# ScalarE's quad copies write four runs of one pixel each instead of two runs of pixel pairs

## The chip, the cores and the metric

The kernel runs on one core of one Trainium2 chip. The metric is device time in microseconds (us), the median of several runs. A profile of one more execution gives the rows that are read here. In it PE is TensorE (PEld its weight loads), DVE is VectorE, ACT is ScalarE, POOL is GpSimd and SP is SyncE, whose queue issues most transfers.

## The reference, cut to what matters

128 images of 3 x 224 x 224 are cut into 8 x 8 patches of 28 x 28 pixels. Every patch is projected to 128 features, gets a position factor, then a windowed attention and a mixture of 16 experts. The change lies in the first step:

```
patches = X.reshape(B, C, 8, 28, 8, 28)
patches = patches.transpose(0, 2, 4, 1, 3, 5).reshape(B, 64, 3 * 28 * 28)
tokens = jnp.einsum('bpi,hi->bph', patches, W) + b          # W: 128 x 2352
...
h = h + attention(layernorm(h)); h = h + moe_and_ffn(layernorm(h))
```

All of it is float32.

## The kernel before, in words

There are three stages. Stage 1 (to about 450 us of the trace) makes tokens, attention and routing for 16 groups of 512 tokens (8 images each); stage 2 runs the experts, stage 3 the last feed-forward layer. The change touches stage 1 alone.

In stage 1 SP loads a group's pixels into `region`, with 84 partitions for the 28 rows of 3 channels and the patch's 28 pixel columns along the free dimension. VectorE moves blocks of the last 7 columns onto unused partitions (`move_block`, L947), so that 21 columns are left to multiply (`MAIN`). For TensorE the 21 columns must be apart, one operand of 256 tokens for each column. ScalarE does that, for each half of a group (256 tokens): `copy_units` writes five quads of four neighbouring columns into `xf` (L632, 128 x 1024 elements each) and the last column into `xlast` (L635, 128 x 256). So a group takes 10 quad copies and 2 copies of a last column. Each such unit raises `xact_ready`.

TensorE's `patch` (L1435) waits for a unit and multiplies each of its columns with that column's weights `wp[:, s]`, adding up over 21 columns in PSUM. The trace has two records of 128x256 for each float32 product, so a quad is 8 records and a last column 2. A unit's buffer is free for the next half when `xunit_used` says that TensorE has read it.

The order on each engine is written by hand and is in order. In one pass of ScalarE's `body` the copies stand between the small steps of the attention: `take_patch` (L640, which takes the finished projection of a group, `hF`), a copy, `take_w` (L681), four copies, `take_x` (L644, L645), the last column and a copy, `take_v` (L677), `take_s` (L665, the softmax's exp), two copies, `take_a` (L673), a copy, `take_z` (L652, `hT`), a copy and the last column, `take_r` (L660), `route_b` (L669). TensorE's `body` has patch units 0 to 11 of the next group between its own transposes (L1440), scores (L1449), values (L1456), gates (L1467), projection (L1511) and attention (L1518). VectorE has the norms, the softmax and the routing between its six block moves of a group.

Of the kernel before, what the change touches and what calls it, by code (L numbers as in the profile page):

```python
# [63 lines left out]
QUADS = MAIN // 4  # L64
UNITS = QUADS + 1
HALVES = 2
HTOK, HIMG = GTOK // HALVES, GIMG // HALVES
# [45 lines left out]
def build(nc, consts, x, tok_w, tok_b, cls_tok, pos, w_c, ln_g, ln_b, r_w, r_b, ew1, eb1, ew2, eb2,  # L113
          sw1, sb1, sw2, sb2, f_g, f_b, fw1, fb1, fw2, fb2, out):
    with ExitStack() as ctx:
        def sb(name, shape, dt=F32):
            return ctx.enter_context(nc.sbuf_tensor(name, shape, dt))
# [89 lines left out]
        h2h, h2l = ([parts[:, 4 * W + (2 * c + u) * EROWS:4 * W + (2 * c + u + 1) * EROWS] for u in range(2)] for c in range(2))  # L207

        xf = sb("xf", [P, QUADS * 4 * HTOK])
        xquad = [xf[:, u * 4 * HTOK:(u + 1) * 4 * HTOK].rearrange("p (q t j) -> p q t j", q=2, j=2) for u in range(QUADS)]  # L210
        xlast = sb("xlast", [P, HTOK])
        eb2_rows = xf[:, 0:E * D]
        shs = [xf[:, E * D + u * SC * GTOK:E * D + (u + 1) * SC * GTOK].rearrange("p (c r) -> p c r", c=SC) for u in range(2)]
# [1521 lines left out]
```

## Time and profile before

| | |
|---|---|
| time, median of 3 runs | 907.61 us (907.56 to 908.23) |
| span of the profiled execution, first to last instruction | 972.0 us |
| PE busy | 896.2 us (92%) |
| ACT busy | 599.5 us (62%) |
| DVE busy | 676.2 us (70%) |
| L1435, matmuls that read `xf` | 314.0 us busy, 1280 records |
| L632, quad copies | 174.0 us busy, 160 instructions |

The profiled execution has no time of its own beside its span, which is 64.4 us above the median. A busy share is an average over the three stages. Matmuls are pipelined: the mean of one record is longer than the distance from one to the next.

### The profile page before, as it was taken

The page shows a single profiled execution, that of the slowest core. Times are in us where ns is not written, and L with a number is a line of the kernel's source. Part 1 is how long each engine was busy: PE and PEld are TensorE (multiplying, and loading weights), DVE is VectorE, ACT ScalarE, POOL GpSimd, SP SyncE. Part 2 cuts the span into 40 slices and gives each one's busy share as a digit, 9 for nine tenths or more (in the row PEclk, how much of TensorE's full clock was granted, in tenths as well). Part 3 has the DMA queues.
Part 4 walks back from the last instruction along what each step waited for, and adds up shares of the span by engine and source line. Part 5 has one row for each costly group of instructions (what it writes and reads, how often), then busy time and mean ns, then how long its engine had stood idle before and what let it go on. Part 6 is the DMA issues. An engine that isn't in the chain of part 4 may idle for free. (4 is left out here: it accounts for less than half of the span.)

```text
span 972.0 us, 22164 instructions
## 1 busy us (share of the span) xinstructions
PE 896.2 (92%) x5920; PEld 801.2 (82%) x5920; DVE 676.2 (70%) x2244; ACT 599.5 (62%) x1064; POOL 438.8 (45%) x374
## 2 busy tenths in 40 slices
PE   2999999989999999999889999999999899789999
PEld 2788888778878888888779889898999899679888
DVE  8377877757877887787556666666676675488884
ACT  3567666656666666777645565555555565477766
POOL 6012554425555545554451445455555464334342
PEclk9999999979999999999879999999999999989999
DMA  9999999977788888767137687777778675334432
GB/s 225 224 221 225 242 247 240 237 205 210 213 228 218 214 216 219 194 216 213 50 105 215 196 227 218 214 219 228 216 224 236 184 221 166 107 82 115 107 103 57
DMA packets 194299, 186.96 MB, mean 192 GB/s; under 512 B 16797, under 2 KB 168698, under 8 KB 194010
## 3 DMA queue, kind: packets, MB, share of 16 engines
q1 hardware_dynamic: 183168, 166.24, 65.2%
q0 software_dynamic: 9376, 19.42, 6.1%
q10 hardware_dynamic: 1722, 0.93, 0.5%
q8 instruction: 12, 0.20, 0.1%
q14 instruction: 21, 0.17, 0.1%
HBM read 150.48 MB, written 36.04 MB: 192 GB/s over the span
## 5 line engine op out<-in xcount | busy, mean ns | idle before, releaser
L1435 PE MATMUL bank<-xf,wp 128*128 128x256 f32 x1280 | 314.0, 394 | 8.4 <-ACT xf L632 5.4
L1435 PEld LDWEIGHTS bank<-xf,wp 128*128 128x128 f32 x1280 | 237.7, 192 | 51.6 <-issue 7.4
L916 POOL DMA_INDIRECT y_tok<-region,dsti x160 | 162.9, 1018 | 164.9 <-DVE region L1268 119.0
L874 POOL TENSOR_TENSOR rstd<-var,neghalf 128x4 f32<-128x4 f32 (+2 forms) x51 | 80.6, 1580 | 287.9 <-DVE var L1030 156.4
L632 ACT ACTIVATE xf<-region 128x1024 f32<-128x1024 f32 x160 | 174.0, 1137 | 18.3 <-DVE region L947 18.3
L890 POOL DMA_INDIRECT z_rows<-z,posg x130 | 157.3, 1210 | 52.5 <-issue 52.2
L798 ACT ACTIVATE region<-bank,cols 128x256 f32<-128x256 f32 x320 | 132.3, 476 | 55.2 <-PE bank L1626 37.2
L1637 PE MATMUL bank<-region 128*128 128x128 f32 x1280 | 156.8, 275 | 1.1 <-DVE region L1268 1.0
L1637 PEld LDWEIGHTS bank<-region 128*128 128x128 f32 x1280 | 150.4, 192 | 1.7 <-issue 1.5
L1626 PE MATMUL bank<-parts 128*128 128x256 f32 x960 | 136.6, 290 | 14.2 <-DVE parts L1279 8.8
L1626 PEld LDWEIGHTS bank<-parts 128*128 128x128 f32 x960 | 119.6, 190 | 25.7 <-issue 19.0
L947 DVE COPY region<-region 32x1792 f32<-32x1792 f32 x96 | 104.8, 1092 | 50.3 <-ACT hT L652 28.9
L788 ACT ACTIVATE region<-bank,cols 128x256 f32<-128x256 f32 x80 | 45.4, 567 | 81.0 <-PE bank L1615 46.5
L1223 DVE CAST parts<-region 128x512 fp32r<-128x512 f32 x80 | 35.4, 443 | 70.9 <-DMA region<-in_L_ffn_ew 56.7
L1684 PE MATMUL bank<-region 128*128 128x128 f32 x520 | 61.7, 277 | 0.0
L1684 PEld LDWEIGHTS bank<-region 128*128 128x128 f32 x520 | 59.4, 192 | 0.9 <-ACT region L819 0.5
L1225 DVE TENSOR_TENSOR parts<-region,parts 128x512 fp32r<-128x512 f32 x80 | 55.6, 694 | 2.8
L1329 DVE SCALAR_TENSOR_TENSOR region<-region,w_all 128x128 f32<-128x128 f32 x130 | 50.3, 446 | 7.6 <-issue 5.3
L1665 PE MATMUL bank<-parts,wparts 128*128 128x512 f32 (+1 forms) x204 | 51.5, 403 | 3.4 <-DVE parts L1368 3.4
L1665 PEld LDWEIGHTS bank<-parts,wparts 128*128 128x128 f32 x204 | 37.5, 195 | 12.0 <-issue 3.6
L834 ACT ACTIVATE region<-region,nmr,rstd 128x128 f32<-128x128 f32 x65 | 26.9, 484 | 30.3 <-DVE nmr L1363 30.3
L819 ACT ACTIVATE region<-bank,cols 128x512 f32<-128x512 f32 (+1 forms) x68 | 40.6, 657 | 3.0 <-PE bank L1665 3.0
(183 smaller groups left out, 1232.3 us busy)
## 6 DMA issues: line engine op xcount, KB each, us to landing
region<-in_x SPq DMA_DIRECT2D x384, 196.0 KB
region<-in_L_ffn_ew SPq DMA_DIRECT2D x160, 256.0 KB
region<-z_rows SPq DMA_DIRECT2D x80, 130.0 KB
region<-y_tok SPq DMA_DIRECT2D x16, 512.0 KB, 3.6
ht_dram<-hT SPq DMA_DIRECT2D x16, 256.0 KB
r_dram<-rr SPq DMA_DIRECT2D x16, 256.0 KB
region<-ht_dram SPq DMA_DIRECT2D x16, 256.0 KB, 5.5
region<-r_dram SPq DMA_DIRECT2D x16, 256.0 KB
```

The costliest lines, as they stand in the source:

```text
L632: ins = act.activation(xquad[i].rearrange("p q t j -> p t q j"), src[:, :, 4 * i:4 * i + 4].rearrange("p t (q j) -> p t q j", j=2), ACT.Copy)
L798: act.activation(ehT[n % 2][:, c], bank[1 + c][:, 0:EROWS], ACT.Silu, bias=bias[c])\
L874: pool.tensor_tensor(dst, var, neghalf[:, 0:var.shape[1]], ALU.pow).then_inc(ready, 1)
L890: pool.indirect_dma_start(z_rows, bass.IndirectOffsetOnAxis(posg[k][:, n:n + 1], 0), z[k][:, t], None).then_inc(z_free[k], 16)
L916: pool.indirect_dma_start(y_tok, bass.IndirectOffsetOnAxis(dsti[n % 2][:, i:i + 1], 0), yout[n % 2][:, i], None).then_inc(y_free[n % 2], 16)
L947: dve.tensor_copy(dst, src).then_inc(block_moved, 1)
L1225: dve.tensor_tensor(w1l[n % 2], w1b[n % 4], w1h[n % 2], ALU.subtract).then_inc(w1l_ready, 1)
L1435: ins = pe.matmul(out_cols, wp[:, s], cols_in, start=s == 0, stop=s == MAIN - 1)
L1626: ins = pe.matmul(bank[1 + c][:, 0:EROWS], w[n % 2][:, c * P:(c + 1) * P], v[n % 2], start=i == 0, stop=i == len(terms) - 1)
L1637: ins = pe.matmul(bank[5 + n % 2][:, i * P:(i + 1) * P], ehT[n % 2][:, c, i * P:(i + 1) * P], w2b[n % 4][:, c], start=c == 0, stop=c == EC ...
L1665: ins = pe.matmul(dst, w[:, c * P:(c + 1) * P], v[:, 0:nt * P], start=i == 0, stop=i == len(terms) - 1)
L1684: ins = pe.matmul(bank[FFD_BANK[k]][:, t * P:(t + 1) * P], ffs[:, c, t * P:(t + 1) * P], fw2_t[:, c], start=c == 0 and t == 0, stop=c == E ...
```

## The change

The view of a quad's buffer is laid out anew. Before, the buffer of 1024 elements held two parts of 512, and each part 256 tokens with two neighbouring columns side by side: a copy wrote two elements (8 bytes), then two elements 512 elements further on. Now the buffer holds four runs of 256 tokens, one for each column: a copy writes one element in each run, 256 elements (1 KB) apart, and then the next token's four. A matmul read every second element of a part; now it reads 256 neighbouring elements. What is computed, the number and order of instructions on every engine and all waits are as before. ScalarE's rows only change their shape, from 128x256x2x2 to 128x256x4.

```diff
         xf = sb("xf", [P, QUADS * 4 * HTOK])
-        xquad = [xf[:, u * 4 * HTOK:(u + 1) * 4 * HTOK].rearrange("p (q t j) -> p q t j", q=2, j=2) for u in range(QUADS)]
+        xquad = [xf[:, u * 4 * HTOK:(u + 1) * 4 * HTOK].rearrange("p (q j t) -> p q t j", q=2, j=2) for u in range(QUADS)]
         xlast = sb("xlast", [P, HTOK])
```

## Rows read from the trace of the kernel before

**Rows 1.** The page: span, busy times, granted clock and DMA in 40 slices.

```profile
span 972.0 us, 22164 instructions
PE 896.2 (92%) x5920; PEld 801.2 (82%) x5920; DVE 676.2 (70%) x2244; ACT 599.5 (62%) x1064; POOL 438.8 (45%) x374
PEclk9999999979999999999879999999999999989999
DMA  9999999977788888767137687777778675334432
```

**Rows 2.** `take_patch`, one per group: how often, and first and last start.

```profile
L640 ACT ACTIVATE fm<-bank,cols x16: 669/687/689, 47.1 to 448.1; 128x512 f32<-128x512 f32 x16
```

**Rows 3.** Windows: length, busy us of PE, PEld, DVE, ACT, POOL, clock, DMA share, GB/s.

```profile
47.06:448.10 401.04, 386.23 (x2157) 330.79 (x2158) 301.67 (x1115) 266.46 (x373) 186.27 (x136) 0.99 0.86 221
...
371.02:397.16 26.14, 25.73 (x148) 22.01 (x147) 20.45 (x77) 17.83 (x26) 13.77 (x10) 1.00 0.87 225
```

**Rows 4.** Groups of instructions by line and shape, PE: mean ns of one.

```profile
L1435 PE MATMUL bank<-xf,wp 128*128 128x256 f32 x1280 | 314.0, 394 | 8.4 <-ACT xf L632 5.4 <-issue 3.1
...
L1435 PE MATMUL bank<-xlast,wp 128*128 128x256 f32 x64 | 19.1, 379 | 0.0
```

**Rows 5.** The same view, ACT: quad copy, last column, a contiguous 256.

```profile
L632 ACT ACTIVATE xf<-region 128x1024 f32<-128x1024 f32 x160 | 174.0, 1137 | 18.3 <-DVE region L947 18.3
...
L635 ACT ACTIVATE xlast<-region 128x256 f32<-128x256 f32 x32 | 21.8, 680 | 0.0
...
L665 ACT ACTIVATE s_t<-s_t 128x256 f32<-128x256 f32 x16 | 6.7, 416 | 17.2 <-DVE s_t L1113 10.1 <-issue 7.1
```

**Rows 6.** Timeline of ACT in the group from 371.02: start, length, row.

```profile
371.02 0.67 ACT L640 ACTIVATE fm<-bank,cols 128x512 f32<-128x512 f32 x1
371.59 1.15 ACT L632 ACTIVATE xf<-region 128x1024 f32<-128x1024 f32 x1
...
373.38 4.18 ACT L632 ACTIVATE xf<-region 128x1024 f32<-128x1024 f32 x4
379.45 0.60 ACT L644 ACTIVATE fm<-bank 128x512 f32<-128x512 f32 x1 [1.90 <-PE bank L1440]
379.95 0.59 ACT L645 ACTIVATE xs<-bank 128x504 f32<-128x504 f32 x1
...
385.03 0.42 ACT L665 ACTIVATE s_t<-s_t 128x256 f32<-128x256 f32 x1 [1.23 <-DVE s_t L1113]
...
389.32 0.60 ACT L673 ACTIVATE fm<-bank 128x512 f32<-128x512 f32 x1 [1.81 <-PE bank L1440]
...
392.08 0.78 ACT L652 ACTIVATE hT<-bank,cols 128x512 f32<-128x512 f32 x1 [1.12 <-PE bank L1440]
...
394.32 1.65 ACT L660 ACTIVATE rr<-h,rs 128x128 f32<-128x128 f32 x4
396.99 0.26 ACT L669 ACTIVATE d<-d 128x72 f32<-128x72 f32 x1 [1.02 <-DVE d L1167]
397.16 0.67 ACT L640 ACTIVATE fm<-bank,cols 128x512 f32<-128x512 f32 x1
```

**Rows 7.** Timeline of PE in the same group.

```profile
373.12 5.57 PE L1435 MATMUL bank<-xf,wp 128*128 128x256 f32 x24
...
381.06 1.05 PE L1449 MATMUL bank<-xs,fm 128*128 128x128 f32 x8
...
384.65 0.59 PE L1435 MATMUL bank<-xlast,wp 128*128 128x256 f32 x2
...
393.17 0.96 PE L1467 MATMUL bank<-rw,hT 128*128 128x16 f32 x8
...
395.87 0.59 PE L1435 MATMUL bank<-xlast,wp 128*128 128x256 f32 x2
```

**Rows 8.** Timeline of DVE in the same group.

```profile
384.57 0.42 DVE L1113 TENSOR_TENSOR s_t<-s_t,mx 128x256 f32<-128x256 f32 x1
...
396.80 0.16 DVE L1167 TENSOR_TENSOR d<-m 128x8 f32<-128x8 f32 x1
```

## The prediction

> **What bounds the kernel now.** I read the page first. TensorE is busy 92% of the span and ScalarE 62%, an average over three unlike stages [rows 1]. The change lies in stage 1 alone, so I took that apart. `take_patch` runs once per group, 16 times from 47.1 to 448.1 us [rows 2]: 15 periods of (448.1 - 47.1) / 15 = 26.7 us each. In the windows TensorE is busy 386 of 401 us there, at a granted clock of 0.99; in the group from 371.02 to 397.16 it is busy 25.73 of 26.14 us and ScalarE 17.83 [rows 3]. So TensorE sets the pace of this stage, and ScalarE has some 8.3 us to spare per group. The DMA share is 0.86 over the stage and near full in its first part [rows 1, 3]; the loads are close behind, but not what a group ends on.
>
> The timelines show where ScalarE's spare time lies: in short waits for the others' steps, 1.90 us before `take_x`, 1.23 before the exp, 1.81 before `take_a`, 1.12 before `hT`, 1.02 before the routing's exp [rows 6]. The last of these waits for VectorE's L1167, which ends at 396.96, 3.79 us after the gates began on TensorE at 393.17 [rows 7, 8]. The next group's `hF` at 397.16 comes right behind it. Whatever delays the gates delays the group.
>
> **The change, part by part.** No instruction is added, removed or moved. Two access patterns change.
>
> *TensorE reads neighbours instead of every second element.* 24 records that read `xf` take 5.57 us [rows 7]; without the last one's length, 0.39 us [rows 4], that is 5.18 / 23 = 0.225 us from one to the next. The two records of `xlast`, which already lies in a run, take 0.59 us [rows 7], with 0.379 us for the second [rows 4]: 0.21 us apart. Both stream 256 columns. So I take 0.01 us off each of the 80 records of a group, 0.8 us per group, 12.8 us over 1280 records. This gain can't be more than that, and it is worth something only where TensorE sets the pace.
>
> *ScalarE writes one element, then hops 1 KB.* No row of before has such a write, so I bound its price. Lower end: nothing. The pairs hop too, 2 KB each, and 1024 elements take 1.137 us where a plain 256 take 0.416 [rows 5]: 0.72 / 768 = 0.94 ns per element, 0.18 us fixed. Upper end, from the reading side: a last column reads single elements 28 apart and takes 0.680 us for 256, against 0.416 for a plain 256 [rows 5]; that is 1.03 ns more per lone element, and on 1024 elements 1.06 us more per copy. Between them stands the nearest row, the pair copy itself, on this engine, buffer and port: if a lone write holds the port as long as a pair does, (1.137 - 0.18) / 512 = 1.87 ns, the copy takes 0.18 + 1024 x 1.87 ns = 2.09 us, **0.95 us more**. It is close to what the lone read costs (1.03 ns on 0.94 is 1.97 ns), so I take it.
>
> The Trainium skill, "SBUF — State Buffer", section "Door 1: The DMA port swizzle", says that memory lines are 16 bytes and that two accesses to a line are needed to hide the latency, so that one access per line pays a penalty. By that rule the new write pays and both layouts of the matmul's read do not, so that TensorE would gain nothing; the 0.225 against 0.21 us speaks against that second half, and no row here shows the first. By this rule the sum below loses only the 0.8 us, which the forecast hardly uses.
>
> **The walk through a group**, with copies of 2.09 us that start 1.97 us apart (now 1.01: four in 4.18 us [rows 6]) and patch units of 8 x 0.215 = 1.72 us. Zero is `hF`'s start, 371.02.
> - First copy from 0.57 to 2.66; TensorE began on it at 2.10 (373.12) and now waits 0.6 us [rows 6, 7].
> - `take_w` and four copies: the next free moment is 10.9. `take_x` starts there, not at 8.43, and `xs` is written at 12.0 instead of 9.5 [rows 6].
> - The scores begin at 12.05, not at 10.04 (381.06) [rows 7]. VectorE's maximum is subtracted 3.93 us after they began (384.99 - 381.06 [rows 7, 8]), at 16.0. ScalarE has done the last column, a copy and `take_v` by then and waits about a microsecond; the exp ends at 16.4.
> - Two copies, done at 18.4 and 20.4. TensorE needs the first for 1.72 us and then 0.6 for the transposes: `take_a` at 20.8 instead of 18.30. A copy until 23.4, `hT` until 24.0.
> - TensorE multiplies that copy's unit from 23.45 to 25.2 and starts the gates, against 22.15 now. VectorE's step follows 3.79 us later at 29.0, the routing's exp adds 0.26, and the next `hF` starts at 29.2 instead of 26.14.
>
> ScalarE's own sum agrees: 17.83 + 10 x 0.95 = 27.3 us busy, and some 2 us of waits that nothing covers (exp 1.1, `take_a` 0.5, the routing's exp). The engine that had slack becomes the bound, and TensorE's 0.8 us vanish in its waits for copies. What is late next is the following group's `hF`; the loads wait for the copies too (`reload_x`), but a longer group gives DMA more time, not less. Against the mean period: 29.2 - 26.7 = 2.5 us, times 15 = **37.5 us**. The first copies before 47 us lie beside cold setup, and the last pass has 6 copies instead of 10; I set the two against each other. Stages 2 and 3 don't touch `xf` with this pattern and stay.
>
> The sum is made in the profiled execution, whose span is 972.0 us; the runs' median is 907.61, 64.4 less, and no row says where. If all 64.4 were spread evenly, the gain in period would shrink to 35 us; if it lay in stage 1's waits, the periods would be near TensorE's own 25.7 us, and 29.2 - 25.7 = 3.5 us times 15 would be 53. I add the 37.5 as it is: 907.6 + 37.5 = **945 us**.
>
> **Rivals.**
> - *A lone write costs no more than one of a pair* (other side). Then only TensorE's part acts: the gates come some 0.7 us earlier, `hF` at 25.4, 0.7 x 16 = 11 us less: **897 us**. For it: pairs already hop and run at 0.94 ns per element. Against: the lone read at 680 ns. It decides below an extra of about 0.3 us per copy.
> - *The price is half as large, 0.55 us per copy, and the two parts cancel.* The same walk with starts 1.57 us apart: `take_x` at 8.9, the scores at 10.05, `take_a` at 18.0, `hT` at 20.3, and the gates at 22.0 against 22.15: **908 us**. This is the point where the sign turns; from there on each 0.1 us per copy costs about 0.75 us per group. The Trainium skill, "Vector Engine (DVE) Microarchitecture Reference", section 5.2, gives for VectorE 1.71 ns per element when the destination hops 4 KiB every element, 1.054 when it is in a run, and no loss for pairs; an estimate in ScalarE's cycles from that page is 0.54 ns more per element, which is this rival. No run here shows VectorE's figure.
> - *A lone write costs as much as the lone read,* 1.06 us per copy. ScalarE is the bound already, so all ten count: 1.1 us more per group than in the forecast, (2.5 + 1.1) x 15 = 54: **962 us**. For it: the row's 680 ns. Against: its hops are of 112 bytes, not of 1 KB, and on the reading side.
> - *TensorE doesn't read faster*, its 0.01 us having another cause. In the forecast that changes little, since TensorE then waits; it takes the gain from the first rival (908 instead of 897).
>
> **How the numbers follow.** By the extra per copy: up to 0.3 us, 0.13 (about 897); 0.3 to 0.5, 0.08 (900 to 905, faster); about 0.55, 0.10 (same); 0.6 to 0.75, 0.15 (912 to 930); 0.75 to 1.0, the forecast, 0.29 (930 to 952); 1.0 to 1.2, 0.17 (952 to 975); more, 0.08. A measurement of this kernel tells 0.2%, 1.8 us, from no change. That makes 0.21 faster, 0.10 same, 0.69 slower. From 900 to 975 the first case and the last fall out, 0.2 in all. If it is slower, 925 to 970 holds most.
>
> **What would show it.** The quad copies' mean: 2.09 us confirms the price, 1.7 the second rival, 1.14 the first. ScalarE busy near 27 of 29 us per group, its waits before `take_x` and `hT` gone; matmuls on L1435 0.215 us apart within a unit, with idle time that ScalarE's L632 ends, where there is next to none now (5.4 us in all [rows 4]). The forecast is wrong if the copies stay below 1.7 us, or if TensorE's granted clock falls in its new waits, which would add to it.

## The result and the profile after

The changed kernel takes 934.68 us (median of 6 runs, 930.75 to 936.30) against 907.62 us (6 runs, 907.11 to 910.35): ratio 1.0291, 95% interval 1.0269 to 1.0312, 27 us slower. 945 was forecast, in a range from 900 to 975.

The first profile, with its span of 972.0 us, was of a disturbed execution, so a second profile of the same kernel before (the first experiment, span 907.4 us) stands beside the changed one from here on.

The busy times on the page of the changed kernel (its span is 928.9 us):

```profile
PE 865.6 (93%) x5920; PEld 787.6 (85%) x5920; DVE 675.0 (73%) x2244; ACT 714.7 (77%) x1064; POOL 433.8 (47%) x374
```

ScalarE's busy time rose from 594.7 us in the second profile of before to 714.7; those of TensorE (865.7 us) and VectorE (676.2 us) hardly changed. The groups of ACT and PE instructions that the change touches (mean ns of one behind the busy time):

```profile
L632 ACT ACTIVATE xf<-region 128x1024 f32<-128x1024 f32 x160 | 308.4, 2020 | 2.0 <-DVE region L947 2.0
...
L635 ACT ACTIVATE xlast<-region 128x256 f32<-128x256 f32 x32 | 21.9, 683 | 0.0
```

```profile
L1435 PE MATMUL bank<-xf,wp 128*128 128x256 f32 x1280 | 306.8, 388 | 21.4 <-ACT xf L632 21.3
```

A quad copy takes 2.020 us instead of 1.137 [rows 5]; a last column, which was not touched, takes the same 0.68. The row still names the shape 128x1024: the new layout shows in the time alone. TensorE now idles 21.3 us before L1435, waiting for copies, where it was 5.4 [rows 4]. Where the time went shows in the windows, first stage 1 from the first to the last `take_patch`, then one group of it, then all the rest (columns as in [rows 3]):

```profile
48.69:452.75 404.06, 382.46 (x2157) 328.38 (x2158) 302.03 (x1114) 378.91 (x372) 180.11 (x136) 1.00 0.83 219
371.32:398.45 27.13, 25.73 (x148) 22.08 (x147) 20.68 (x77) 25.49 (x26) 13.41 (x10) 1.00 0.78 217
452.75:928.90 476.15, 455.96 (x3656) 436.33 (x3654) 343.47 (x1084) 308.26 (x665) 236.65 (x221) 0.99 0.63 184
```

The same three in the second profile of before:

```profile
46.18:427.32 381.14, 379.04 (x2157) 327.77 (x2158) 303.45 (x1116) 266.95 (x374) 186.50 (x136) 1.00 0.92 234
249.46:274.81 25.35, 25.35 (x148) 22.08 (x147) 20.72 (x77) 17.95 (x25) 13.57 (x10) 1.00 0.96 253
427.32:907.40 480.08, 460.26 (x3656) 440.20 (x3654) 344.07 (x1084) 308.52 (x665) 234.56 (x221) 0.98 0.63 183
```

Stage 1's 15 periods grew from 381.14 to 404.06 us, that is from 25.41 to 26.94 us each, and 2.5 us came ahead of them. The rest of the program did not grow. (The two spans differ by 21.5 us, the medians by 27: the profiled execution of the changed kernel was the fastest of its runs, 930.75 us.) Before, TensorE was busy in 25.35 of 25.35 us: it set the pace. After, it is busy 25.73 of 27.13 and ScalarE 25.49: neither is full.

The timeline shows how the two now wait for each other. ScalarE in the group from 371.32 us of the changed kernel (start, length, row; in brackets the idle time ahead):

```profile
371.32 0.69 ACT L640 ACTIVATE fm<-bank,cols 128x512 f32<-128x512 f32 x1
...
374.24 7.43 ACT L632 ACTIVATE xf<-region 128x1024 f32<-128x1024 f32 x4
381.45 0.65 ACT L644 ACTIVATE fm<-bank 128x512 f32<-128x512 f32 x1
...
385.70 0.42 ACT L665 ACTIVATE s_t<-s_t 128x256 f32<-128x256 f32 x1 [0.21 <-DVE s_t L1113]
...
390.84 0.60 ACT L673 ACTIVATE fm<-bank 128x512 f32<-128x512 f32 x1 [0.99 <-PE bank L1440]
...
393.12 0.74 ACT L652 ACTIVATE hT<-bank,cols 128x512 f32<-128x512 f32 x1
...
398.03 0.26 ACT L669 ACTIVATE d<-d 128x72 f32<-128x72 f32 x1 [0.29 <-DVE d L1167]
398.45 0.69 ACT L640 ACTIVATE fm<-bank,cols 128x512 f32<-128x512 f32 x1
```

TensorE in the same group:

```profile
373.14 0.60 PE L1440 MATMUL bank<-cst,fm 128*128 128x128 f32 x4
373.99 1.99 PE L1435 MATMUL bank<-xf,wp 128*128 128x256 f32 x8 [0.24 <-ACT xf L632]
376.30 3.79 PE L1435 MATMUL bank<-xf,wp 128*128 128x256 f32 x16 [0.31 <-ACT xf L632]
...
380.36 1.89 PE L1435 MATMUL bank<-xf,wp 128*128 128x256 f32 x8
382.70 1.15 PE L1449 MATMUL bank<-xs,fm 128*128 128x128 f32 x8 [0.45 <-ACT xs L645]
...
392.37 0.60 PE L1440 MATMUL bank<-cst,z 128*128 128x128 f32 x4
393.36 1.99 PE L1435 MATMUL bank<-xf,wp 128*128 128x256 f32 x8 [0.40 <-ACT xf L632]
395.19 0.96 PE L1467 MATMUL bank<-rw,hT 128*128 128x16 f32 x8
...
397.81 0.59 PE L1435 MATMUL bank<-xlast,wp 128*128 128x256 f32 x2
```

And TensorE in the group from 249.46 us of the second profile of before:

```profile
251.29 0.60 PE L1440 MATMUL bank<-cst,fm 128*128 128x128 f32 x4
251.72 5.57 PE L1435 MATMUL bank<-xf,wp 128*128 128x256 f32 x24
...
259.37 1.05 PE L1449 MATMUL bank<-xs,fm 128*128 128x128 f32 x8
...
269.24 0.60 PE L1440 MATMUL bank<-cst,z 128*128 128x128 f32 x4
269.68 1.97 PE L1435 MATMUL bank<-xf,wp 128*128 128x256 f32 x8
271.48 0.96 PE L1467 MATMUL bank<-rw,hT 128*128 128x16 f32 x8
...
274.18 0.59 PE L1435 MATMUL bank<-xlast,wp 128*128 128x256 f32 x2
```

The waits that ScalarE had of 1.90 us before `take_x` and 1.12 before `hT` [rows 6] (1.61 and 0.67 in the second profile) are gone. TensorE has four instead: before the first unit, the second, the scores (for `xs`), and unit 9. Idle time counts from a record's modelled end; the loss is better read from start to start. The first unit follows 0.85 us after the transposes instead of 0.43 in the second profile of before. The second comes 2.31 us after the first, where eight records 0.215 us apart take 1.72. The scores come 2.34 us after the unit ahead of them, also instead of 1.72, and unit 9 follows the transposes of `z` after 0.99 us instead of 0.44. That makes 0.4 + 0.6 + 0.6 + 0.6 us in the four places. Records behind a wait come more slowly (eight take 1.99 us there and 1.89 without a wait), which adds some 0.4. Less the 0.8 of shorter reads, the sum is the 1.78 us that this group takes longer.

### The profile page after: what moved, and what is told of

Its sections match the earlier page's. It is cut to its first block and busy times, and to the rows that moved or that the text cites. A ratio compares the mean times of both kernels' runs of the same rounds, so it can differ in the third digit from the quotient of the medians.

```text
span 928.9 us, 22164 instructions
## 1 busy us (share of the span) xinstructions
PE 865.6 (93%) x5920; PEld 787.6 (85%) x5920; DVE 675.0 (73%) x2244; ACT 714.7 (77%) x1064; POOL 433.8 (47%) x374
## 5 line engine op out<-in xcount | busy, mean ns | idle before, releaser
L1435 PE MATMUL bank<-xf,wp 128*128 128x256 f32 x1280 | 306.8, 388 | 21.4 <-ACT xf L632 21.3
L632 ACT ACTIVATE xf<-region 128x1024 f32<-128x1024 f32 x160 | 308.4, 2020 | 2.0 <-DVE region L947 2.0
L1435 PEld LDWEIGHTS bank<-xf,wp 128*128 128x128 f32 x1280 | 236.2, 192 | 65.2 <-ACT xf L632 32.1
L890 POOL DMA_INDIRECT z_rows<-z,posg x130 | 150.4, 1157 | 44.2 <-issue 43.6
L798 ACT ACTIVATE region<-bank,cols 128x256 f32<-128x256 f32 x320 | 125.4, 475 | 21.7 <-PE bank L1626 21.2
L1626 PE MATMUL bank<-parts 128*128 128x256 f32 x960 | 133.8, 289 | 0.4 <-DVE parts L1279 0.4
L788 ACT ACTIVATE region<-bank,cols 128x256 f32<-128x256 f32 x80 | 45.2, 564 | 85.0 <-PE bank L1615 81.9
```

The lines of the kernel that those rows point to most:

```text
L632: ins = act.activation(xquad[i].rearrange("p q t j -> p t q j"), src[:, :, 4 * i:4 * i + 4].rearrange("p t (q j) -> p t q j", j=2), ACT.Copy)
L798: act.activation(ehT[n % 2][:, c], bank[1 + c][:, 0:EROWS], ACT.Silu, bias=bias[c])\
L890: pool.indirect_dma_start(z_rows, bass.IndirectOffsetOnAxis(posg[k][:, n:n + 1], 0), z[k][:, t], None).then_inc(z_free[k], 16)
L1435: ins = pe.matmul(out_cols, wp[:, s], cols_in, start=s == 0, stop=s == MAIN - 1)
L1626: ins = pe.matmul(bank[1 + c][:, 0:EROWS], w[n % 2][:, c * P:(c + 1) * P], v[n % 2], start=i == 0, stop=i == len(terms) - 1)
```

## The experiments

The theory from the prediction: a lone write costs ScalarE 0.9 us more per quad copy, ScalarE becomes the bound, and what TensorE gains is lost in waits.

**The kernel before, unchanged.** 

> The kernel before, unchanged, for a profile whose span lies near its runs' 907.6 us. If stage 1 alone carries the loss of 27 us, its 15 periods average about 27.1 - 27/15 = 25.3 us here, and stages 2 and 3 take as long as in the changed kernel (from the last take_patch at 452.8 to the end at 928.9: 476 us). Rival: the periods are 26.7 us as in the first profile, and the loss lies elsewhere.

It took 907.64 us (ratio 1.0001, 0.9980 to 1.0021). `take_patch` in it:

```profile
L640 ACT ACTIVATE fm<-bank,cols x16: 669/687/688, 46.2 to 427.3; 128x512 f32<-128x512 f32 x16
```

(427.3 - 46.2) / 15 = 25.4 us per period, against the 26.7 of [rows 2]. The loss lies in stage 1.

**TensorE's half alone.**

```diff
+        xread = [... .rearrange("p (q j t) -> p q t j", q=2, j=2) ...]      # xquad stays in pairs
-                        cols_in = xquad[i][:, s % 4 // 2, :, s % 2] if i < QUADS else xlast[:, :]
+                        cols_in = xread[i][:, s % 4 // 2, :, s % 2] if i < QUADS else xlast[:, :]
```

> ScalarE writes pairs as before, TensorE reads four runs of neighbours (so it multiplies other columns than the reference: only the time counts). This is TensorE's half of the change alone. My theory, that a read of neighbours is 0.01 us shorter per record and that TensorE sets the pace while ScalarE has slack: copies 1.14 us, records 0.215 us apart, 8 to 13 us less than before, 895 to 900. Rival, that TensorE's reading is worth nothing because another chain sets the period: 906 to 909.

900.52 us, ratio 0.9926 (0.9906 to 0.9947): 6 us less than the kernel before in the same runs (906.65), and just outside the 895 to 900 of the expectation. Three units in a row, which took 5.57 us in the second profile of before, the transposes behind them, and the step of VectorE that writes `xh` for these:

```profile
299.85 5.35 PE L1436 MATMUL bank<-xf,wp 128*128 128x256 f32 x24
305.28 0.63 PE L1441 MATMUL bank<-cst,xh 128*128 128x128 f32 x4
```

```profile
304.02 1.11 DVE L1022 TENSOR_SCALAR xh<-h,mv,rstd 128x128 f32<-128x128 f32 x4 [1.16 <-POOL rstd L875]
```

0.22 us less over 23 distances, 0.01 us each, as taken from the two kinds of record in [rows 4, 7]. Of 80 x 0.01 = 0.8 us per group the time shows half: 6 us. The rival, no gain, is out. In this group the other half is lost before the scores: `xh` is ready at 305.13, so the transposes come 5.43 us after the first unit, and they came after 5.41 in the kernel before (at 257.13). TensorE reads faster and then waits for VectorE.

**ScalarE's half alone.** `xquad` in runs for the writes, the view of before for TensorE's reads.

> ScalarE writes four runs, one element each, as in the changed kernel; TensorE reads every second element as before (again other columns than the reference). ScalarE's half alone. My theory, that ScalarE's copies set the period and TensorE waits for them: copies 2.02 us, records 0.225 us apart, 935 to 943, little above the changed kernel's 934.7, because part of TensorE's extra 0.8 us per group lies in its waits. Rival, that ScalarE is not the bound and TensorE's records still count in full: 934.7 + 13 = 947.

940.79 us, ratio 1.0373 (1.0346 to 1.0400), inside the forecast of 935 to 943. But it is 6 to 7 us above the changed kernel: TensorE's shorter reads are worth about as much when ScalarE is slow as when it is fast. "Lost in waits" was wrong for about half of them. The two half-changed kernels compute other tokens, which could change the later stages, but what sets them apart lies in stage 1: the periods are 25.06 and 27.41 us long, and from the last `take_patch` on they take 478.1 and 475.9 us.

| | TensorE reads every second | TensorE reads neighbours |
|---|---|---|
| ScalarE writes pairs | 907.6 (before) | 900.5, ratio 0.993 |
| ScalarE writes lone elements | 940.8, ratio 1.037 | 934.7, ratio 1.029 (the change) |

**Runs for seven quads of ten.**

```diff
+        RUNS = (3, 4, 6, 7, 8, 9, 10)
+        xquad = [xrun[n % UNITS] if n in RUNS else xpair[min(n % UNITS, QUADS - 1)] for n in range(HALVES * UNITS)]
```

`xrun` and `xpair` are the views of the changed kernel and of the kernel before; `n` counts the twelve units of a group, and both engines take `xquad[n]`.

> Runs for seven of a group's ten quads (units 3, 4, 6, 7, 8, 9, 10), pairs for units 0, 1 and 2, the same for writing and reading. Seven copies of 2.02 us and three of 1.14 leave ScalarE 18 + 7 x 0.78 = 23.5 us busy per group, below the period of before. My theory, a threshold: nothing is lost up to there and TensorE's 7 x 0.08 = 0.56 us per group are won, 899 to 907. Rival, that each slow copy costs its share: 907.6 + 0.7 x 27 = 926.

924.17 us, ratio 1.0176 (1.0150 to 1.0202). The threshold falls: ScalarE is busy 23.40 of 26.23 us in a group, and still some 17 us are lost, about what the rival said. Some 3 us of it come ahead of the first `take_patch` (at 49.3 us instead of 46.2), the rest in the periods. TensorE's timeline shows where:

```profile
260.25 5.58 PE L1438 MATMUL bank<-xf,wp 128*128 128x256 f32 x24
...
274.15 1.99 PE L1438 MATMUL bank<-xf,wp 128*128 128x256 f32 x8 [0.48 <-ACT xf L635]
...
279.15 1.99 PE L1438 MATMUL bank<-xf,wp 128*128 128x256 f32 x8 [0.40 <-ACT xf L635]
```

Only the units 7 and 9 are waited for; units 0 to 2, in pairs again, run through in 5.58 us. ScalarE copies both just behind a step that waits for others (the exp, `take_a`), and TensorE takes them at once. So neither theory fits as it stood, and a new one follows: the place decides.

**The two places alone, and five others.** The same edit with `RUNS = (7, 9)` and with `RUNS = (3, 4, 6, 8, 10)`.

> Runs for units 7 and 9 alone, the two that TensorE waited for. By the new theory they carry nearly all of the loss of the run with seven: about 1.2 us per group less 2 x 0.07, 15 times, 16 us: 920 to 925. Rival, each slow copy costs its share: 907 + 0.2 x 27 = 912.

> Runs for units 3, 4, 6, 8 and 10 of a group, pairs for the others. In the run with seven slow copies TensorE waited before units 7 (0.48 us) and 9 (0.40 us) and before no other slow one. My new theory: a slow copy costs where TensorE takes its unit as soon as it is written, and nothing where ScalarE copies ahead; each run layout gives TensorE back 0.07 us. So 5 x 0.07 x 15 = 5 us less than before: 900 to 904. Rival, each slow copy costs its share of the 27 us: 907 + 0.5 x 27 = 920.

Two slow copies: 923.48 us, ratio 1.0172 (1.0151 to 1.0193), 16 us. Five: 908.92, ratio 1.0018 (1.0004 to 1.0031), 1.6 us. Net of what TensorE gains, two copies cost ten times as much as five others, and as much as the seven. The rival's shares (912 and 920) are out. With two slow copies TensorE waits in the same two places:

```profile
273.87 1.99 PE L1438 MATMUL bank<-xf,wp 128*128 128x256 f32 x8 [0.20 <-ACT xf L635]
...
278.88 1.99 PE L1438 MATMUL bank<-xf,wp 128*128 128x256 f32 x8 [0.34 <-ACT xf L635]
```

while ScalarE, with only two copies 0.9 us longer, waits 1.63 us before `take_x` in the same group, nearly as before:

```profile
266.08 0.60 ACT L647 ACTIVATE fm<-bank 128x512 f32<-128x512 f32 x1 [1.63 <-PE bank L1443]
```

The five missed the 900 to 904 of the expectation, in two ways: TensorE waits before unit 10 as well, now that it comes there sooner, and the first `take_patch` comes at 49.5 us instead of 46.2.

```profile
273.88 1.99 PE L1438 MATMUL bank<-xf,wp 128*128 128x256 f32 x8 [0.24 <-ACT xf L635]
```

```profile
L643 ACT ACTIVATE fm<-bank,cols x16: 687/689/691, 49.5 to 428.6; 128x512 f32<-128x512 f32 x16
```

**What the price belongs to.** The four runs of a quad 5 KB apart instead of 1 KB:

```diff
+        xquad = [xf.rearrange("p (q j v t) -> p v q t j", q=2, j=2, v=QUADS)[:, u] for u in range(QUADS)]
```

> The changed kernel with the four runs of a quad 5 KB apart instead of 1 KB (the buffer holds a run of each quad, then the next). If the price belongs to a lone element whatever the hop, copies of 2.02 us and the changed kernel's 934.7. If a longer hop costs less, copies below 1.8 us and 905 to 920; by the Trainium skill's table for VectorE (Vector Engine (DVE) Microarchitecture Reference, section 5.2) a copy would take about 1.7 us, an estimate.

The buffer of before, but a token's four elements in another order:

```diff
-  activation(xquad[i].rearrange("p q t j -> p t q j"), src[...].rearrange("p t (q j) -> p t q j", j=2), ACT.Copy)
+  activation(xquad[i].rearrange("p q t j -> p t j q"), src[...].rearrange("p t (q j) -> p t j q", j=2), ACT.Copy)
```

> The buffer of before, in pairs, and TensorE reads as before; ScalarE only writes a token's four pixels in another order, one in the first part, one in the second (2 KB apart), and then the two beside them. If what costs is that two writes in turn don't go to neighbours, copies of 2.02 us and about 940, as with the write half alone. If it is the number of separate places, two instead of four, copies near 1.14 us and 907.

The changed buffer, written run by run, so that the reads are the lone ones:

```diff
-  activation(xquad[i].rearrange("p q t j -> p t q j"), src[...].rearrange("p t (q j) -> p t q j", j=2), ACT.Copy)
+  activation(xquad[i].rearrange("p q t j -> p q j t"), src[...].rearrange("p t (q j) -> p q j t", j=2), ACT.Copy)
```

> The changed buffer, but ScalarE writes one run to its end, then the next: the writes go to neighbours and each read is a lone element 112 bytes after the last. By the last column's row (0.680 us for 256, 1.86 ns each after 0.2 us fixed) a copy takes 0.2 + 1024 x 1.86 ns = 2.1 us, no better than lone writes: 935 to 942. If lone reads are cheaper in a long copy, it shows below 2.0 us.

The copies of the three (min, median and max ns):

```profile
L632 ACT ACTIVATE xf<-region x160: 1962/2020/2080, 22.2 to 449.3; 128x1024 f32<-128x1024 f32 x160
```

```profile
L632 ACT ACTIVATE xf<-region x160: 1984/2039/2097, 22.8 to 458.9; 128x1024 f32<-128x1024 f32 x160
```

```profile
L632 ACT ACTIVATE xf<-region x160: 2062/2114/2190, 21.8 to 464.0; 128x1024 f32<-128x1024 f32 x160
```

The times: 933.26 (ratio 1.0279, 1.0261 to 1.0298), 943.60 (1.0399, 1.0375 to 1.0423), 950.38 us (1.0471, 1.0447 to 1.0495). A hop of 5 KB costs the same as one of 1 KB, so a cheaper long hop is out. With it goes, for ScalarE, the estimate of 1.7 us from the Trainium skill's table for VectorE (Vector Engine (DVE) Microarchitecture Reference, section 5.2). Two places instead of four cost the same, in the very buffer that takes 1.137 us when it is written pair by pair. But that copy also reads a token's pixels in the order 0, 2, 1, 3, so its price can lie in the reads; that two places are as dear as four for writes alone is not shown. The changed kernel has lone writes with reads in order, the third copy lone reads with writes in order, and each pays by itself: all the copies fit one rule, that what counts on either side is whether two elements in turn are neighbours. Lone reads cost about as much as lone writes, a little more, as the last column's row said (2.11 us against the 2.1 worked out). The time of this kernel is above the 935 to 942 of its expectation: it has 16 us more than the changed kernel. The length of a copy, 0.09 us more, hides part of it; four copies in a row, the changed kernel's 7.43 us above, take here

```profile
302.50 8.09 ACT L632 ACTIVATE xf<-region 128x1024 f32<-128x1024 f32 x4
```

so that one starts (8.09 - 2.11) / 3 = 1.99 us after the other instead of 1.80: these copies overlap by 0.12 us, as the pair copies do (four in 4.18 us [rows 6]), and those of the changed kernel by 0.22.

**A mixture that gains.** `RUNS = (3, 4, 6, 8)`, then `(6, 8)`, then the four with the first group left in pairs:

```diff
+        xall = [xpair[min(n % UNITS, QUADS - 1)] for n in range(HALVES * UNITS)]
...
-  xquad[n]
+  (xall if isinstance(g, int) and g == 0 else xquad)[n]
```

> Runs for units 3, 4, 6 and 8. The run with five lost 0.35 us per group before unit 10, which TensorE took at once; without it 4 x 0.07 us per group are won, period 25.1 us against 25.35, 4 us in all. But the first take_patch of the run with five came at 49.5 us against 46.2, so slow copies 3 and 4 may cost up to 3 us once, before the first group: 902 to 907. Rival, each slow copy costs its share: 907 + 0.4 x 27 = 918.

> Runs for units 6 and 8 alone. 2 x 0.07 us per group won, 2 us, and nothing lost before the first group, which starts as before: 904 to 907. If the first group's delay in the run with five came from units 3 and 4, take_patch first starts near 46.5 us here and later in the run with four.

> Runs for units 3, 4, 6 and 8 of every group but the first, whose twelve copies stand in a row with TensorE right behind and stay in pairs. The run with four in all groups had its first take_patch at 48.7 us, against 46.2 of before. If that delay came from the first group's slow copies it goes, and the gain grows from 2 us to about 4: 903 to 905. Rival, it had another cause: 905.5 as before.

Four: 905.50 us, ratio 0.9976 (0.9964 to 0.9989). Two: 908.67, ratio 1.0010 (0.9999 to 1.0022); its expected gain of 2 us did not show in the time. Its first `take_patch` came at 47.1 us, not near 46.5, so units 6 and 8 delay the first group too, by about 0.9 us of the 2.5. Four from the second group on: 903.36, ratio 0.9946 (0.9927 to 0.9964), 4 to 5 us below before, and the first `take_patch` is back near its place:

```profile
L643 ACT ACTIVATE fm<-bank,cols x16: 671/687/690, 48.7 to 425.4; 128x512 f32<-128x512 f32 x16
```

```profile
L644 ACT ACTIVATE fm<-bank,cols x16: 670/687/690, 46.8 to 425.0; 128x512 f32<-128x512 f32 x16
```

The first is of the four in all groups, the second of the last kernel: 48.7 against 46.8 us. This version beats both kernels; it was timed against before, on one chip, and not against the other mixtures in the same runs.

## Why the prediction was right or wrong

The sign was right, and so was the main mechanism: lone writes make ScalarE's copies longer, and TensorE waits for them. The size was too large, 37.5 us forecast and 27 measured, and it came as near as it did because two errors partly cancelled.

- **The price of a lone write.** 0.95 us per copy, taken from the pair copy's row [rows 5]; measured 2.020 - 1.137 = 0.88. The nearest row was the right one; that a lone write holds the port as long as a pair does fits the size, and no run shows it as the reason. Both rivals with a lower price are out (copies of 1.14 or 1.7 us), and so is the lone read's 1.06 as the price of writes, though only just: lone reads measured 2.11 us.
- **The walk.** This is where the size failed. Counted from `take_patch`, the changed kernel's `take_x` comes at 10.1 us (10.9 forecast), the scores at 11.4 (12.05), `take_a` at 19.5 (20.8), the gates at 23.9 (25.2) and the next `hF` at 27.1 (29.2). Three terms were wrong. The start-to-start distance of copies was put at 1.97 us; it is (7.43 - 2.02) / 3 = 1.80. The 3.93 us from the scores' start to the end of the subtracted maximum were carried over as a constant; they are 2.96 in the changed kernel. VectorE shows why, first in the second profile of before, then in the changed kernel:

```profile
259.21 2.21 DVE L947 COPY region<-region 32x1792 f32<-32x1792 f32 x2
261.45 0.86 DVE L1110 TENSOR_TENSOR s_t<-bank,cst 64x256 f32<-64x256 f32 x2
```

```profile
381.07 2.21 DVE L947 COPY region<-region 32x1792 f32<-32x1792 f32 x2
383.89 0.86 DVE L1110 TENSOR_TENSOR s_t<-bank,cst 64x256 f32<-64x256 f32 x2 [0.62 <-PE bank L1449]
```

Before, the scores were done first and VectorE was still moving blocks; in the changed kernel the moves are done and VectorE waits for the later scores. The third term is a path that the kernel normally does not take. The 3.79 us from the gates to VectorE's L1167, with the routing's exp and `hF` right behind, were read from the first profile. In the second profile of before L1167 ends 2.80 us after the gates, in the changed kernel 2.81, so the change shortened nothing here. And `hF` waits for TensorE:

```profile
274.12 0.16 DVE L1167 TENSOR_TENSOR d<-m 128x8 f32<-128x8 f32 x1
```

```profile
274.81 0.69 ACT L640 ACTIVATE fm<-bank,cols 128x512 f32<-128x512 f32 x1 [0.23 <-PE bank L1435]
```

TensorE's last unit ends at 274.77, 0.04 us before `hF`; in the changed kernel it ends at 398.40, 0.05 us before. What sets the period behind the gates is TensorE's own work in both kernels.

- **The base.** 26.7 us per period came from the first profile; in the second it is 25.4. Of the 64.6 us between the two spans of before, 19.9 lie in the fifteen periods, 43.8 behind them and 0.9 ahead. The prediction gave both ends (35 and 53 us for the loss). The lower base raises the loss, the shorter walk lowers it by more: growth per period is 1.53 us measured, 2.5 forecast. That they cancel in part is luck: the walk's 29.2 us against the true base would have made 3.8 us per period, 57 in all. The 2.5 us ahead of the first `take_patch`, which the prediction set against a shorter last pass, come on top of the periods.
- **The clock.** In the periods the granted clock was 1.00 in both kernels, which is the 2.4 GHz level, so it did not fall in TensorE's new waits. Ahead of the first `take_patch` it was 0.89 against 0.96; the run with four slow copies comes as late (48.7 us) at 0.96, so the 2.5 us are not the clock's.
- **"The engine that had slack becomes the bound, and TensorE's 0.8 us vanish."** Half wrong. ScalarE is busy 25.49 of 27.13 us (27.3 forecast) and still waits; the shorter reads are worth 6 of 12 us with either kind of write, as the four kernels show. The period is a chain that goes to and fro between the two engines, and TensorE's records lie on it in both cases.
- **The rule that TensorE would gain nothing** (the Trainium skill, "SBUF — State Buffer", "Door 1: The DMA port swizzle") is refuted for this read: two elements per 16 bytes cost 0.225 us per record, four 0.215. Its other half, that lone accesses pay, agrees with 2.02 against 1.14 us.
- **0.75 us per group for each 0.1 us per copy** beyond the turning point at 0.55, from the walk, was too steep: the measured 0.88 would have cost 2.5 us per group, and 1.53 were lost. A mean over copies is the wrong measure besides: two of the ten alone, made slow, cost 16 us.

## What to carry to other kernels

When a layout moves a cost from the engine that sets the pace to one with slack, the busy shares don't say whether the slack can be used. Look in the timeline for the places where the pacing engine takes a result as soon as it is written: there most of the delay counts (two copies 0.88 us longer in 15 periods are 26 us, and 16 were lost), and elsewhere the same slow copy is nearly free. Where both layouts can stand side by side, choose per place, and leave the pipeline's filling out.

## What was not expected of the hardware

- On ScalarE the price of writing a float32 element without a neighbour is about 0.86 ns over the pair's, with hops of 1 KB and of 5 KB alike: copies of 1024 took 2.020 us, against 1.137 in pairs. Lone reads 112 bytes apart took 2.114. With hops of 2 KB, where the reads were out of order as well, it was 2.039.
- TensorE pays for reading every second float32 element: 0.225 against 0.215 us per 256 columns, at a granted clock of 1.00, which is the 2.4 GHz level.
